# Causal linear attention in a decoder block: leaving out the scores of late keys by early queries, with 32x64 and 64x32 array tiles

## The reference

```python
q, k, v = (x @ qkv_w.T + qkv_b).split_heads()      # 16 heads of 16
q = relu(q) + 1e-6
k = relu(k) + 1e-6
kv    = cumsum(k[..., :, None] * v[..., None, :], axis=tokens)
k_cum = cumsum(k, axis=tokens)
num = einsum('bhld,bhlde->bhle', q, kv)
den = maximum(einsum('bhld,bhld->bhl', q, k_cum), 1e-6)
out = (num / den) @ out_w.T + out_b
```

## Time and profile before

| | us |
|---|---|
| median of 3 executions | 380.3 |
| lowest and highest | 379.59, 382.1 |
| span of the profiled execution, first to last instruction | 377.9 |
| start-up before the first numerators, in it | 35.7 |
| tile loop, first to last numerators, in it | 239.5 |
| last steps, feed-forward part and experts, in it | 102.7 |

### The profile page before, as it was taken

The page is one execution under the profiler, slowest core; times in us unless marked ns, Lnnn a source line. Parts: engine busy times, 40 slices in busy tenths (PEclk is TensorE's granted clock), DMA queues, the critical chain, the costliest instruction groups (busy, mean ns, idle before and its releaser), DMA issues. The chain is left out here.

```text
span 377.9 us, 10670 instructions
## 1 busy us (share of the span) xinstructions
PE 356.6 (94%) x3514; PEld 255.6 (68%) x3514; DVE 296.1 (78%) x922; ACT 162.6 (43%) x394; POOL 279.1 (74%) x414
## 2 busy tenths in 40 slices
PE   8999999999999999999999999999899989998781
PEld 4566677777677777767777777778676556655451
DVE  2588788898989898888898878886756588799462
ACT  2463553454455346436436524442456435331120
POOL 5338987766777866877867789898978888578455
PEclk9999999999999999999999999999999999999897
DMA  8993881200300120032121013003000233148750
GB/s 255 328 308 88 251 245 22 66 16 16 72 31 16 35 53 16 19 83 87 55 49 39 25 25 67 16 20 80 16 31 28 73 97 111 57 146 283 220 181 23
DMA packets 39309, 34.50 MB, mean 91 GB/s; under 512 B 4505, under 2 KB 38456, under 8 KB 39256
## 3 DMA queue, kind: packets, MB, share of 16 engines
q1 hardware_dynamic: 36392, 29.54, 27.7%
q0 software_dynamic: 1312, 3.37, 2.9%
q10 hardware_dynamic: 1552, 0.92, 0.9%
HBM read 17.55 MB, written 12.60 MB: 80 GB/s over the span
## 5 line engine op out<-in xcount | busy, mean ns | idle before, releaser
L1650 POOL TENSOR_TENSOR s_t<-s_t,causal 128x512 f32<-128x512 f32 x63 | 78.9, 1273 | 15.6 <-ACT s_t L961 15.4
L539 PE MATMUL bank<-h1t,w_qkv 128*128 128x512 f32 x112 | 52.9, 595 | 0.4 <-DVE x L1220 0.3
L1207 DVE TENSOR_TENSOR s_t<-sbank,causal 128x512 f32<-128x512 f32 x65 | 43.5, 671 | 1.1 <-PE sbank L560 1.0
L1642 POOL TENSOR_TENSOR state_wide<-state,own_pair 128x256 f32<-128x256 f32 x28 | 18.9, 676 | 25.5 <-DVE state L1198 24.4
L961 ACT ACTIVATE s_t<-sbank 128x512 f32<-128x512 f32 x63 | 33.7, 587 | 7.8 <-PE sbank L560 7.8
L560 PE MATMUL sbank<-arena 32*128 32x256 f32 x512 | 36.7, 400 | 0.0
L599 PE MATMUL bank<-s_t,vp 128*32 128x128 f32 x1024 | 34.6, 275 | 1.1 <-DVE s_t L1207 0.4
L546 PE MATMUL bank<-w_qkv,h1t 128*128 128x256 f32 x128 | 34.2, 389 | 0.0
L1658 POOL TENSOR_TENSOR rr<-ve,neg_half 128x3 f32<-128x3 f32 x36 | 31.9, 887 | 3.0
L684 PE MATMUL bank<-w_out,attn_t 128*128 128x256 f32 x128 | 33.6, 385 | 0.5 <-DVE attn_t L1288 0.5
L778 PE MATMUL sbank<-h1t,w 128*128 128x512 f32 x72 | 33.0, 596 | 0.5 <-ACT h1t L961 0.5
(11 more groups left out here) (231 smaller groups left out, 831.5 us busy)
## 6 DMA issues: line engine op xcount, KB each, us to landing
rden_t<-rden SPq DMA_DIRECT2D x64, 64.0 KB
rows<-x SPq DMA_DIRECT2D x32, 128.0 KB, 1.7
x<-in_x SPq DMA_DIRECT2D x7, 512.0 KB, 8.6
out<-x SPq DMA_DIRECT2D x7, 512.0 KB
we<-in_we SPq DMA_DIRECT2D x1, 2048.0 KB
xmask<-in_mask POOLq DMA_DIRECT2D x2, 616.0 KB, 10.3
rows<-empty SPq DMA_DIRECT2D x1, 1032.0 KB, 5.2
we<-in_we SPq DMA_DIRECT2D x1, 1024.0 KB
```

Source lines behind the costliest of these rows:

```text
L539: mm = pe.matmul(dst[:, :], w_qkv[:, ch, cb * P:(cb + 1) * P], h1t[:, g % 3, ch, :], start=(ch == 0), stop=(ch == CH - 1))
L1207: dve.tensor_tensor(s_t[:, r, :, :], sbank[r][:, :].rearrange("p (s q) -> p s q", s=4), causal[:, :].unsqueeze(1).to_broadcast([P, 4, P]), ...
L1650: pool.tensor_tensor(s_t[:, r, :, :], s_t[:, r, :, :], causal[:, :].unsqueeze(1).to_broadcast([P, 4, P]), ALU.mult)\
```

## The change

The 128 keys of a tile and its 128 queries are each cut into an early and a late half of 64. Late keys by early queries are always masked out, and this quarter of the scores is no longer computed, copied, masked or multiplied by values. What is left of a score bank is 384 of 512 columns.

- `scores`: a product now has 64 keys as columns of weights. 8 products stream 2 x 128 queries (early keys), 8 more stream 2 x 64 (late keys by late queries). The two chunks of heads (`ch`) go to the two 64-column halves of the array, so that eight 32x64 tiles are in use, two per score bank.
- For that chunk 1 has the halves of its keys exchanged: early keys stand on partitions 64 to 127. ScalarE makes turned copies for it, `h1r` from `h1t` (`turn_h1`, 256 columns) and `k1r` from the keys (`turn_k1`, 128 columns), each once per tile, after the eviction of h1; the values are computed in two halves of 128 features, the second from `h1r`.
- `numerators` is split: `early_numerators` runs 16 products with 64 rows, 32 columns and 128 queries, `late_numerators` 16 with 64 queries. They use eight 64x32 tiles; chunk 0 accumulates in `bank[1]` (columns 256 to 383), chunk 1 in `bank[3]`. The late part stands behind the state update and waits for the end of the early part.
- Bank 1 is also that of the cross-attention scores, so `from_state` and the early numerators now wait for VectorE's maximum (`max_done`), and the transpose of the probabilities waits for `attn_ready`. VectorE's maximum and its negative are moved ahead of `v_evict`.
- Masks are 128x384 (`allowed`). A few tables of the last part share memory with others, and three semaphores are merged.

```diff
+        allowed = sb("allowed", [P, 3, HB])
...
-        s_t = sb("s_t", [P, RG, 4, P])
+        scored = sb("scored", [P, RG * 4 * P])
+        s_t = scored[:, 0:RG * 3 * P].rearrange("p (r g s n) -> p r g s n", r=RG, g=3, s=2)
...
-        bank = [ctx.enter_context(nc.psum_tensor(f"bank{i}", [P, 512], F32)) for i in range(4)]
+        banks = ctx.enter_context(nc.psum_tensor("bank", [P, 4, 512], F32))
+        bank = [banks[:, i, :] for i in (0, 2, 1, 3)]
...
+        def turns_h1(t):
+            return t + 1 if t < 2 else 2 * t
+
+        def turns_k1(t):
+            return min(2 * t + 3, 2 * NT)
+
+        def turned(ap):
+            return ap.rearrange("p c (k n) -> p c k n", k=2)[:, :, ::-1, :]
+
+        def region(r):
+            return sbank[r][:, 0:3 * P].rearrange("p (g s n) -> p g s n", g=3, s=2)
+
+        def numerators_at(ch):
+            return bank[1 + 2 * ch]
 
         def starts(t):
             return t % TPB == 0
@@ -463,7 +495,7 @@
...
             def values(t):
                 wait(pe, h1t_ready, t + 1)
-                for ch in range(CH):
-                    mm = pe.matmul(v_place(t), h1t[:, (t // GT) % 3, ch, tok(t)], w_qkv[:, ch, 2 * D:3 * D],
-                                   start=(ch == 0), stop=(ch == CH - 1))
+                wait(pe, turn_ready, turns_h1(t))
+                for of in range(CH):
+                    for ch in range(CH):
+                        mm = pe.matmul(v_place(t)[:, of * P:(of + 1) * P],
+                                       h1r[:, t % 2, ch, :] if of else h1t[:, (t // GT) % 3, ch, tok(t)],
+                                       w_qkv[:, ch, 2 * D + of * P:2 * D + (of + 1) * P],
+                                       start=(ch == 0), stop=(ch == CH - 1), skip_group_check=True)
                 mm.then_inc(v_done, 1)
 
             def scores(t):
...
-                for ch in range(CH):
-                    for r in range(RG):
-                        rows = slice(32 * r, 32 * r + 32)
-                        both = sbank[r][:, 2 * ch * P:2 * (ch + 1) * P].rearrange("p (s n) -> p s n", s=2)
-                        mm = pe.matmul(both, kt(slot, ch)[rows, tok(t)], qpair(slot, ch)[rows, :, tok(t)],
-                                       start=True, stop=True)
+                for c in range(2):
+                    for ch in range(CH):
+                        for r in range(RG):
+                            rows = slice(32 * r, 32 * r + 32)
+                            at = side(ch if c == 0 else 1 - ch)
+                            keys = kt(slot, ch)[rows, part(t, c)]
+                            if c == 0:
+                                queries = qpair(slot, ch)[rows, :, tok(t)].rearrange("p s (k n) -> p k s n", k=2)
+                                mm = pe.matmul(region(r)[at, 0:2 + ch:1 + ch, :, :], keys, queries,
+                                               start=True, stop=True, skip_group_check=True)
+                            else:
+                                mm = pe.matmul(region(r)[at, 1 + ch, :, :], keys, qpair(slot, ch)[rows, :, part(t, 1)],
+                                               start=True, stop=True, skip_group_check=True)
                 mm.then_inc(s_done, 1)
...
                 wait(pe, h1t_ready, min(t + 1 + AHEAD + 1, NT))
                 wait(pe, x2_ready, t - 2)
                 wait(pe, wide_ready, updates(t))
+                wait(pe, max_done, t - 1)
                 for ch in range(CH):
-                    pe.matmul(bank[3][:, ch * P:(ch + 1) * P],
+                    pe.matmul(numerators_at(ch)[:, OUT],
                               state_wide[:, (t - 1) % 2, ch, :, :].rearrange("p r e -> p (r e)"),
-                              qall(slot, ch)[:, tok(t)], start=(ch == 0), stop=False, skip_group_check=True)
-
-            def numerators(t):
+                              qall(slot, ch)[:, tok(t)], start=True, stop=False, skip_group_check=True)
+
+            def early_numerators(t):
                 wait(pe, h1t_ready, min(t + 1 + AHEAD + 1, NT))
                 wait(pe, x2_ready, t - 2)
                 first = starts(t)
+                wait(pe, max_done, t - 1)
                 wait(pe, s_masked, on_dve(t + 1))
                 wait(pe, s_pooled, on_act(t + 1))
                 wait(pe, v_ready, t + 1)
-                for ch in range(CH):
-                    for par in range(2):
+                for par in range(2):
+                    for ch in range(CH):
                         for r in range(RG):
                             head = HC * ch + 2 * r + par
-                            v_of = vp[:, t % 3, head // 2, 32 * par:32 * par + 32]
-                            mm = pe.matmul(bank[3][32 * r:32 * r + 32, ch * P:(ch + 1) * P], v_of,
-                                           s_t[:, r, 2 * ch + par, :], start=(first and ch + par == 0),
-                                           stop=(ch + par == 2), skip_group_check=True)
+                            mm = pe.matmul(numerators_at(ch)[32 * r:32 * r + 32, OUT],
+                                           vp[side(ch), t % 3, head // 2, 32 * par:32 * par + 32],
+                                           s_t[side(ch), r, 0:2 + ch:1 + ch, par, :], start=(first and par == 0),
+                                           stop=False, skip_group_check=True)
+                mm.then_inc(early_done, 1)
+
+            def late_numerators(t):
+                pe.wait_ge(early_done, t + 1)
+                for par in range(2):
+                    for ch in (1, 0):
+                        for r in range(RG):
+                            head = HC * ch + 2 * r + par
+                            mm = pe.matmul(numerators_at(ch)[32 * r:32 * r + 32, D + HB:D + P],
+                                           vp[side(1 - ch), t % 3, head // 2, 32 * par:32 * par + 32],
+                                           s_t[side(1 - ch), r, 1 + ch, par, :], start=False,
+                                           stop=(par == 1), skip_group_check=True)
                 mm.then_inc(num_done, 1)
 
             def step(pe, i):
...
                     wait(pe, ktok_ready, K)
+                    wait(pe, turn_ready, turns_k1(K))
                     wait(pe, den_ready, -(-K // GT))
                     wait(pe, v_ready, K + 1)
                     for ch in range(CH):
-                        mm = transpose(bank[2][:, ch * P:(ch + 1) * P], kt((K // GT) % 2, ch)[:, tok(K)])
+                        mm = transpose(bank[2][:, ch * P:(ch + 1) * P], k1r[:, K % 2, :] if ch else kt((K // GT) % 2, 0)[:, tok(K)])
                     mm.then_inc(ktr_done, 1)
...
                 if is_tile(M):
-                    numerators(M)
+                    early_numerators(M)
                 if is_tile(K) and (K + 1) % TPB:
                     wait(pe, ktok_ready, K + 1)
                     wait(pe, x2_ready, i - 3)
@@ -657,12 +715,14 @@
                     wait(pe, v_ready, K + 1)
                     for ch in range(CH):
                         for r in range(RG):
-                            col = D + ch * 2 * HD
+                            col = ch * 2 * HD
                             v_of = vp[:, K % 3, RG * ch + r, :].rearrange("p (q e) -> p q e", q=4)[:, 0:4:3, :]
                             mm = pe.matmul(bank[3][32 * r:32 * r + 32, col:col + 2 * HD],
                                            k_tok[:, K % 2, ch * P + 32 * r:ch * P + 32 * r + 32], v_of,
-                                           start=True, stop=True, skip_group_check=True)
+                                           start=not is_tile(M), stop=True, skip_group_check=True)
                     mm.then_inc(st_done, 1)
+                if is_tile(M):
+                    late_numerators(M)
                 if is_tile(K) and K % GT == 0:
                     denominators(K // GT)
                 if i == 0:
@@ -672,6 +732,8 @@
...
                 if is_tile(B):
                     wait(pe, exp_done, B + 1)
+                    if is_tile(M):
+                        wait(pe, attn_ready, M + 1)
                     transpose(bank[1][0:KX, 0:P], prob[:, B % 2, :]).then_inc(ptr_done, 1)
...
+            def turn_h1(t):
+                wait(act, h1t_ready, t + 1)
+                wait(act, v_done, t - 1)
+                copy(h1r[:, t % 2, :, :].rearrange("p c (k n) -> p c k n", k=2), turned(h1t[:, (t // GT) % 3, :, tok(t)]))\
+                    .then_inc(turn_ready, 1)
+
+            def turn_k1(t):
+                wait(act, qk_ready, 4 * (t // GT) + 2)
+                wait(act, ktr_done, t - 1)
+                copy(k1r[:, t % 2, :].rearrange("p (c k n) -> p c k n", c=1, k=2),
+                     turned(kt((t // GT) % 2, 1)[:, tok(t)].unsqueeze(1))).then_inc(turn_ready, 1)
...
-                        copy(flat(s_t[:, r, :, :]), sbank[r][:, :]).then_inc(s_copied, 1)
+                        copy(s_t[:, r, :, :, :].rearrange("p g s n -> p (g s n)"), sbank[r][:, 0:3 * P]).then_inc(s_copied, 1)
...
```

(37 more changed lines are left out.)

61 lines of the change are left out of this document (30 added, 31 removed).

## The result

The changed kernel takes 396.6 us (median of 4 executions, 395.7 to 399.1) against 380.3 us, a ratio of 1.043 (1.039 to 1.048). It is slower, and above the forecast range, which ended at 391. The profiled execution spans 395.2 us, 17.3 more than before. The first numerators start at 35.7 us in both traces; the last ones at 290.27 instead of 275.16, so 15.1 us are lost in the tile loop.

A forecast was written before the change was run, and what follows sets the result against it. TensorE's instruction list was taken to bound each step. Terms -7.7 + 4.8 - 0.6 (values) + 4.9 - 1.0 + 0.5 = +0.9 us gave about 381.3 us from the median of 380.3; range 373.5 to 391.

The forecast's parts named there:

- Array prices: TensorE in the tile loop: scores save 7.7 us, numerators with state update add 4.8 us, changes of shape priced in full.
- Both rivals about the array: 64x32 to 128x32 changes are free: 374.0 us, 15%; eight tiles don't run side by side: 422 or 391 us, 14%.
- The new wait: `from_state` waits for VectorE's maximum before writing bank 1: 0.14 us in 19 steps, +4.9 us in all.
- the third rival: Maximum or late `attn_t` holds TensorE 0.3 us more in 28 steps than costed: 389.7 us, 10%.
- The 1.0 us taken back: Five steps where VectorE was late lost some 1.6 us; shorter masks and the earlier maximum win back 1.0 us.
- this wait costs nothing in a normal step: TensorE's wait for `attn_t`: VectorE's product takes 0.4 us and finishes before TensorE is through with the scores.
- Start-up: Step 0: `turn_k1(0)` ahead on ScalarE and VectorE building `allowed` cost +0.5 us, between 0 and 1.

The follow-up runs named there:

- experiment 4: Changed kernel with VectorE's maximum of the cross scores (and its negative) moved ahead of the second masking; 399.1 us, ratio 1.048.
- experiment 2: Kernel before the change with each numerator product cut into two of 64 queries and each score product into two of 128, old tile shapes; 388.0 us, ratio 1.018.
- experiment 3: Changed kernel with 640 products of the late numerators' shape (2560 instructions) run in a row after the warm-up; 445.0 us in one execution.
- experiment 7: Changed kernel with 352 already fulfilled waits on TensorE, maximum before second masking, numerators as early by early plus all keys by late queries; 403.9 us.
- experiment 9: Changed kernel, TensorE's program shifted by 158 instructions in the warm-up: 399.1 us; second kernel adds re-cut numerators and mostly earlier maximum: 393.2 us.
- experiment 6: Changed kernel with 352 already fulfilled waits added to TensorE's program to shift the borders between blocks of 256 instructions; 413.6 us, ratio 1.087.
- 10: 203 tiny products ahead of numerators in eight tiles: 393.4 us with re-cut numerators and mostly earlier maximum, 402.9 us on the changed kernel alone.
- experiment 5: Changed kernel with numerators cut as early keys by early queries, then all keys by late queries in 128x32 tiles; 394.3 us, ratio 1.036.
- experiment 8: Changed kernel with late keys' scores behind the out products and VectorE adding x before first masking: 411.4 us; with re-cut numerators and earlier maximum: 403.2 us.

## Why the prediction was wrong

**Array prices: right.** To the next start, in us, forecast and measured: scores 0.84 and 0.84, early numerators 0.60 and 0.60, state update 0.26 and 0.26, late numerators 0.39 and 0.38. In the steps with denominators +0.25 forecast, +0.24 measured; without state update +0.12 and +0.17 (0.80 and 0.39 for 1.01 before). Both rivals about the array are out: changes between 64x32 and 128x32 cost in full, and eight tiles run side by side.

**The new wait: right in place, too small in size.** The maximum starts at 194.74, 1.13 us after the block's eviction at 193.61; forecast 1.17. But the value products take 0.94 us and not 0.89 where nothing is waited for (experiment 4, 0.49 and 0.45), and in the changed kernel 1.09, and `from_state` behind the wait takes 0.61 instead of 0.54 us. It takes 0.54 in tile 1, where there was no wait, so the 0.07 goes with the wait, probably because after it the first weights are loaded in the open: they start 0.03 us ahead of the product, at 195.10, and 0.11 us where there is no wait (experiment 4). Together a wait costs 0.23 where I had 0.14. The sum of a normal step, -0.24 + 0.11 + 0.03 + 0.16 + 0.07 = +0.13 us, is the one read (8.04 against 7.91), and I had 0.00. Over some 21 steps that is 2.8 us. This is a small part of the third rival, which had 0.3 us a step. At the loop's end the same wait is longer, as VectorE is later there:

```profile
280.93 0.67 PE L693 MATMUL bank<-w_score,h2t 128*128 128x77 f32 x4 [0.26 <-ACT h2t L1023]
282.44 0.68 PE L627 MATMUL bank<-arena,state_wide 128*128 128x128 f32 x4 [0.84 <-DVE mx L1340]
```

In the earlier trace rows the distance was 0.50; here it is 1.51, and in the step after it 1.39, so +1.9 us for the two where I had 0.7.

**The 1.0 us taken back: wrong.** Before the change five steps lost 0.40, 0.41 and three times 0.11 us, 1.1 us together and not 1.6 as I had it. The three small losses are gone, but tiles 8 and 16 now lose 0.56 us ahead of the out products, for 0.40 before, so nothing is won. VectorE does come earlier, but the transpose of the probabilities, which ran ahead of the out products in the earlier trace rows, now waits for `attn_t` too, since it writes bank 1. VectorE's product in tile 16,

```profile
173.09 0.39 DVE L1369 TENSOR_TENSOR attn_t<-bank,rden_t 128x256 f32<-128x256 f32 x1
```

ends at 173.48, and the transpose starts only at 173.63. I had written that this wait costs nothing in a normal step, and did not ask what it does in the steps in which the eviction is late. **Start-up** cost nothing that can be seen; the loop starts at 35.7 us as before.

**What was missing: the supply of instructions.** The terms above, with the sizes measured, add up to about 6 of the 15.1 us lost in the loop. The other 9.1 were in none of the terms and in none of the rivals; without them the time would have been near 387.5 us, inside the range, though 6 above the sum. The sum counted what each instruction costs the array and took for granted that it is there. The number was on the page, and in my working: 3514 records before, 52 more in every step, and four instructions for each product in single precision (two passes, each a weight load and a matmul). What I used of it was that records start 0.007 us apart, as an argument for the array; that the program then has to come at 256 instructions in 2.4 us I did not ask. The rows of before could not show the limit, since its fastest burst is 128 instructions in 2.2 us, but they could have shown that the burst would become denser than anything in the trace. That experiment 2, which only cuts the old products into more instructions, shows the same stretches is the shortest proof; experiment 3 gives a rate, at the lower clock.

The Trainium skill, "Trainium Architecture — The Big Picture", section "The software stack", says that the instruction streams are brought into each engine's memory when the program is loaded. The trace does not agree: 43 packets of 16 KB arrive during the execution, and TensorE stands still where one is late.

**What stays open.** What starts the fetch of a block; why the packet of tile 1 came 4 us behind the border before it with no wait in the way (the DMA engines were busy with loads then); and whether a kernel with the cheaper step of experiment 7, 7.76 us, can beat the kernel before. Without the stretches its loop would end where that of the kernel before does or a little earlier (in the second kernel of experiment 9 the loop is 10.6 us longer than before, of which the stretches are some 11), so what there is to win is small. None of the versions measured beats the kernel before.

## What to carry to other kernels

Count instructions as well as columns: when products are cut into smaller tiles, compare the densest run of instructions with what the trace shows to be sustained, here 256 in about 3.5 us on TensorE (at the lower clock), and look at the row of the instruction queue. An idle stretch with "issue" behind it and no wait in the code, at instruction numbers that agree modulo 256, is the mark of a late block; a saved tenth of a microsecond elsewhere in such a step is given back there. And where a new wait is put in front of a product, add a little to its price beyond the time waited, here 0.07 us.

## What the runs showed of the hardware that was not expected

- TensorE's program arrives in packets of 16 KB, 256 instructions, during the execution. In a dense stretch a block took 3.45 us at best (1.1 until the next packet starts, 2.33 from there to its first instruction), at a granted clock of 0.50, and 5.7 to 6.7 us while the DMA engines were 0.8 to 1.0 busy (experiment 3).
- An instruction that only waits, for something long there, cost TensorE 29 to 55 ns in four steps that had 29 to 64 of them, and long matmuls around it did not hide it (experiment 6).
- Pauses of 1.4 to 2.1 us without a matmul were followed by some microseconds at half clock (4: 2.11 us, 6: 1.97, 9: 1.42, 10: 1.79 and 2.02), so a gap of 2.5 us between weight loads cost 5.9 (experiment 6). Others were not (1.86 us in the changed kernel, 2.27 in experiment 5), so the length of the pause alone does not decide.
- Each change between 128-column products and 32x64 tiles in the middle of other work cost 0.1 to 0.15 us on either side (experiment 8).
